# Distance factors of four batches at once on 32 partitions each, in a kernel of two graph layers with layernorms

## The reference, cut to what matters

```
s = x @ w_se.T + b_se                      # 512 x 3 for each batch
sq = sum(s * s, axis=-1)
dist = sq[:, :, None] + sq[:, None, :] - 2 * einsum('bnd,bmd->bnm', s, s)
A = exp(-dist) * mask
x_nmp = einsum('bnm,bmd->bnd', A, relu(x @ w_msg.T + b_msg))
```

## Time and profile before

| | |
|---|---|
| runs | 359.60, 358.53, 354.52 us; median 358.53 us |
| the profiled execution | 354.5 us, of it the span 352.4 us |
| PE busy | 335.6 us, 95% |
| DVE busy | 316.2 us, 90% |
| ACT busy | 237.3 us, 67% |
| DMA queue q1 | 33.49 MB, 31.1% of 16 engines' span |

### The profile page before, as it was taken

How to read it: one execution, slowest core, us unless ns; L and a number is a source line. 1 busy time by engine, 2 the same in 40 slices (tenths; PEclk the granted TensorE clock), 3 DMA queues, 4 the chain that set the end, 5 groups by cost and what they waited for, 6 DMA issues and landing times. The chain is left out here.

```text
span 352.4 us, 6224 instructions
## 1 busy us (share of the span) xinstructions
PE 335.6 (95%) x1769; PEld 274.6 (78%) x1769; DVE 316.2 (90%) x553; ACT 237.3 (67%) x409; POOL 93.2 (26%) x151
## 2 busy tenths in 40 slices
PE   4889999999999999999999999999999999999891
PEld 1577778987889688977989688977898688967580
DVE  2999999999999999999999999999999999987633
ACT  4382675748856696748865796659684885967842
POOL 4740001605050502323050504141140406050222
PEclk9989999999999999999999999999999999999998
DMA  6913341514044222604162312603161403421012
GB/s 183 327 24 119 91 138 46 173 32 150 19 114 147 64 88 56 195 25 149 31 182 63 121 33 72 198 20 129 45 201 30 149 17 93 139 74 37 0 32 60
DMA packets 31096, 34.00 MB, mean 96 GB/s; under 512 B 4919, under 2 KB 18271, under 8 KB 31079
## 3 DMA queue, kind: packets, MB, share of 16 engines
q1 hardware_dynamic: 30054, 33.49, 31.1%
q10 hardware_dynamic: 1024, 0.30, 0.3%
HBM read 24.85 MB, written 4.46 MB: 83 GB/s over the span
## 5 line engine op out<-in xcount | busy, mean ns | idle before, releaser
L1319 POOL TENSOR_TENSOR base<-mv,vscale 128x4 f32<-128x4 f32 x16 | 7.0, 437 | 232.3 <-DVE mv L1448 225.5
L715 PE MATMUL p_outer<-t_h,w_l 128*128 128x344 f32 x131 | 41.1, 330 | 0.6 <-DVE w_l L1526 0.6
L715 PE MATMUL p_outer<-t_h,w_h 128*128 128x344 f32 x131 | 41.0, 328 | 0.2 <-DVE rz L1523 0.2
L1416 DVE TENSOR_TENSOR am<-am,adj 128x512 f32<-128x512 f32 x64 | 39.9, 683 | 0.0
L1582 DVE TENSOR_TENSOR am_l<-am,am_h 128x2048 fp32r<-128x2048 f32 x15 | 34.3, 2286 | 1.8 <-ACT am_h L1172 1.8
L715 PE MATMUL p_middle<-t_h,w_h 128*128 128x344 f32 x90 | 28.6, 329 | 0.0
L1172 ACT ACTIVATE am_h<-am 128x2048 fp32r<-128x2048 f32 x15 | 28.5, 1901 | 0.0
L715 PE MATMUL p_middle<-t_h,w_l 128*128 128x344 f32 x90 | 28.0, 322 | 0.0
L715 PEld LDWEIGHTS p_outer<-t_h,w_h 128*128 128x128 f32 x131 | 24.3, 188 | 2.5 <-issue 0.6
L715 PEld LDWEIGHTS p_outer<-t_h,w_l 128*128 128x128 f32 x131 | 25.0, 195 | 1.2 <-DVE w_l L1526 0.9
L1131 ACT ACTIVATE yoo<-yn,nb,rs 128x128 f32<-128x128 f32 x63 | 25.9, 484 | 0.0
(11 more groups left out here) (381 smaller groups left out, 1010.0 us busy)
## 6 DMA issues: line engine op xcount, KB each, us to landing
adj<-adjT SPq DMA_DIRECT2D x64, 256.0 KB, 3.5
xpad<-xT SPq DMA_DIRECT2D x17, 256.0 KB, 3.1
out<-yoo SPq DMA_DIRECT2D x16, 256.0 KB, 2.3
crossed<-left SPq DMA_DIRECT2D x31, 48.0 KB
left<-left SPq DMA_DIRECT2D x30, 48.0 KB
right<-left SPq DMA_DIRECT2D x30, 48.0 KB
wc<-w_c SPq DMA_DIRECT2D x2, 384.0 KB, 6.6
wraw<-g_w SPq DMA_DIRECT2D x1, 640.0 KB
```

The lines of the kernel that those rows point to most:

```text
L715: return nc.tensor.matmul(out_, w, x, start=start, stop=stop, skip_group_check=True)
L1319: TT(base[:, 0:CH], mv[:, :, 1], vscale[:, 0:CH], ALU.mult)
L1416: TT(am[:, c, :], am[:, c, :], adj[:, c, :], ALU.mult).then_inc(s_am[c], 1)
```

## The change

1. **Rows.** One contraction now has KD = 30 rows, arranged so that the right side is the left side with its two halves of 15 rows exchanged. Only one side is computed, on 32 partitions for a batch, so four batches fit into 128 partitions. `rows` issues one matmul of 32 columns for each batch. In the head it makes batches 0 and 1, in batch 1 batches 2 and 3 (partitions 64 to 127), and in batches 3, 7 and 11 the next four. Batches 5, 9 and 13 no longer have `rows`, `rows_factor`, `rows_val`, `rows_high` or `rows_left`. For the two batches whose x isn't in `xin` yet, SP loads x a second time into `xr` (2 x 256 KB, in batches 2, 6 and 10).
2. **Right side.** DVE makes the right side by a stream shuffle of `left` within each 32 partitions into `crossed` (which is the memory of `val`), after `x_l` in an odd batch, five times in all.
3. **Distances.** `dist` uses two row quarters, the batch's own and its neighbour's, in turn: matmuls 0 and 2 on one, 1 and 3 on the other. SP issues three copies for each batch instead of six: one of the left rows, two of the right rows after the shuffle. Copies for the third and fourth batch of a group of four are issued in the next two batches.
4. **Head.** The `rowb` operation moves behind the steps of the first convolution. Batch 0 gets its right side through the shuffle and an ACT copy (`rights[0]`) instead of a DMA. On the ACT queue the two DMAs of `brow` become one.

```
-KD = 24
+KROW = 15
+KD = 2 * KROW
+MIRROR = [(r + KROW) % KD if r < KD else r for r in range(32)]
...
+            def spread_factors(v, event=None):
+                g, p = v % 4, v % 2
+                rows_l, rows_r = full(left[32 * g:32 * g + KD, :]), crossed[32 * g:32 * g + KD]
+                sp.dma_start(full(lefts[p][32 * other(g):32 * other(g) + KD, :]), rows_l).then_inc(s_right[p], 16)
+                if event is not None:
+                    after(sp, s_crossed, event)
+                for h in (g, other(g)):
+                    sp.dma_start(full(rights[p][32 * h:32 * h + KD, :]), rows_r).then_inc(s_right[p], 16)
...
-                if v % 2 and before(b, B - 2):
-                    after(sp, s_left, n.pair(1))
+                if v == 2:
+                    after(sp, s_rows, n.quad(0))
                     for q in range(2):
-                        spread_factors(q)
+                        sp.dma_start(xr[:, q, :], xT[b + 4 + q, :, :]).then_inc(s_xr, 16)
+                if v == 3 or static(b, 1):
+                    after(sp, s_left, n.quad(0)); after(sp, s_d, n(1))
+                    spread_factors(v + 1, n.quad(0))
+                    spread_factors(v + 2)
+                elif not isinstance(b, int):
+                    if v != 2:
+                        after(sp, s_d, n(0))
+                        spread_factors(v + 2)
...
+            def row_group(g, x_):
+                return mm(p_gh[32 * g:32 * g + 32, :], wrow[:], x_)
+
+            def rows(v, extra=False):
                 for q in range(2):
-                    last = mm(p_gh[64 * q:64 * q + 64, :], wrow[:], xin[:, (v + q) % 4, :])
+                    last = row_group((v + q) % 4, xin[:, (v + q) % 4, :])
+                if extra:
+                    for q in range(2):
+                        last = row_group(2 + q, xr[:, q, :])
                 last.then_inc(s_rows, 1)
...
-                at, other = 64 * (v % 2), 64 - 64 * (v % 2)
-                for c, (lhs, rhs, row) in enumerate(((left, crossed, at), (crossed, left, at + 32),
-                                                     (left2, right2, other), (left2, right2, other + 32))):
-                    last = mm(banks[c][:], lhs[row:row + KD, D * c:D * c + D], rhs[row:row + KD, :])
+                for c in range(CH):
+                    g, p = v % 4, v % 2
+                    h, lhs, rhs = other(g) if c % 2 else g, lefts[p] if c % 2 else left, rights[p]
+                    last = mm(banks[c][:], lhs[32 * h:32 * h + KD, D * c:D * c + D], rhs[32 * h:32 * h + KD, :])
                 last.then_inc(s_d, 1)
...
+            def rows_crossed(at, e):
+                nc.vector.stream_shuffle(crossed[at], full(left[at, :]), MIRROR).then_inc(s_crossed, 1)
...
-                dve.wait_ge(s_brow, 32); dve.wait_ge(s_cst, 16)
-                TS(rowb[:], brow[:], cst[:, C_ROW:C_ROW + 1], cst[:, C_ROW + 1:C_ROW + 2], ALU.mult, ALU.add).then_inc(s_rowb, 1)
...
-                rows_val(o, 0)
-                rows_left(o, 0)
+                dve.wait_ge(s_brow, 16); dve.wait_ge(s_cst, 16)
+                TS(rowb[:], brow[:], cst[:, C_ROW:C_ROW + 1], cst[:, C_ROW + 1:C_ROW + 2], ALU.mult, ALU.add).then_inc(s_rowb, 1)
+                rows_val(slice(0, 64), 1, 0)
+                rows_left(slice(0, 64), 1, 0)
+                dve.wait_ge(s_left, 1)
+                rows_crossed(slice(0, 64), 1)
...
+                    if v == 3 or static(b, 1):
+                        rows_left(part_of(v), n.quad(0), n(1))
+                        after(dve, s_left, n.quad(0))
                     x_low(v, n, 3)
+                    if v == 3 or static(b, 1):
+                        rows_crossed(part_of(v), n.quad(0))
                     inner_low(n)
```

More of the change, by code:

```diff
@@ L33 @@
 XS = N3 + 1
[L37 removed]
+KROW = 15
+KD = 2 * KROW
+MIRROR = [(r + KROW) % KD if r < KD else r for r in range(32)]
 def dist_rows():
[L42 to L55 removed]
+    first, second = [], []
+    for k in range(3):
+        first += [(k, 0.0, 1.0, 0), (k, 0.0, 1.0, 0), (k, 0.0, 1.0, 1), (k, -1.0, 0.0, 0), (k, -1.0, 0.0, 1)]
+        second += [(k, 0.0, 1.0, 0), (k, 0.0, 2.0, 1), (k, 0.0, 1.0, 1), (None, 0.0, 1.0, 0), (None, 0.0, 1.0, 0)]
+    return first + second, []
 (V_G1, V_B1, V_M1, V_V1, V_G2, V_B2, V_M2, V_V2, V_IR, V_IZ, V_IN, V_HR, V_HZ, V_HN) = range(14)
@@ L86, in constants @@
     c[:, C_ID:C_ID + D] = np.eye(D)
-    for side, rows in enumerate(dist_rows()):
-        for r, (_, alpha, beta, low) in enumerate(rows):
-            for b in range(2):
-                c[64 * b + 32 * side + r, C_ROW:C_ROW + 3] = alpha, beta, -low
+    for r, (_, alpha, beta, low) in enumerate(dist_rows()[0]):
+        for g in range(4):
+            c[32 * g + r, C_ROW:C_ROW + 3] = alpha, beta, -low
     c[:, C_ONE] = 1
@@ L586, in x_count, with other, part_of @@
             return (b - (v + k) % 4) * 4 + 16
+        def other(g):
+            return g + 1 - 2 * (g % 2)
+        def part_of(v):
+            return slice(64, 128) if v == 1 else slice(0, 128)
         def static(b, value):
@@ L937, in odd @@
                     g_pe.combine(pe, mm)
-                if more:
-                    after(pe, s_val, n.pair(1))
+                if v == 3 or static(b, 1):
+                    after(pe, s_val, n.quad(0))
                 after(pe, s_ghb, n(0)); gate(p_gh, "n", 2, xb_h, xb_l, True, True).then_inc(s_gx, 1)
@@ L1092, in first @@
                 act.wait_ge(s_rowb, 1)
-                act.wait_ge(s_rows, 1)
-                A(ab, p_gh[:], ACT.Identity, bias=rowb[:, 0:1], scale=cst[:, C_ROW:C_ROW + 1]).then_inc(s_ab, 1)
-                act.wait_ge(s_val, 1)
-                A(val_h[:], val, ACT.Copy).then_inc(s_valh, 1)
+                rows_factor(slice(0, 64), 1)
+                rows_high(slice(0, 64), 1)
                 middle_high(o)
```

101 lines of the change are left out of this document (45 added, 56 removed).

## The result

The two kernels were compared in 20 runs each. The median is 356.98 us after the change (356.08 to 361.75) against 354.89 us before (354.07 to 359.60); the ratio of the compared runs is 1.0054 with a 95% interval of [1.0031, 1.0076].

What follows compares the result with a forecast made beforehand. PE was taken to set the time, with DVE close behind. Rows -3.6 + 1.1, distances 2.5 + 1.5, shuffle 1.2 and head 1.0 made +3.7 us: 358.2 or 362.2, stated as 360.2, range 355 to 366.

Steps and rivals of the forecast that it cites:

- rows, batches 5, 9, 13: These batches lose a 1.21 us slot: 3 x 1.21 = 3.6 us saved, of which 1.1 us is lost again.
- shuffle, batches 3, 7, 11: 0.65 us of DVE each, also in batch 1; stalls PE 0.3 at the last convolution sum, 4 x 0.3 = 1.2.
- head itself: In the head, DVE's chain with the moved rowb and the shuffle makes the w_l of 21.28 come 1.0 us late.
- the distances' term: dist on two quarters: eight instances outside the even batches cost 0.31 each, 2.5 us; seven even ones 0.22, 1.5 us.
- So PE sets the time: In the loop PE sets the time with almost no slack; DVE's gains are worth nothing where PE is later.
- the rival of rounds that don't overlap: In dist the second round costs a whole slot of 0.43, 1.8 us more: 360.0 and 364.0; chance 0.06.
- quarters used in turn run one by one: Slow rival: dist costs 0.77, 6.9 us more than summed: 365.1 and 369.1; chance 0.07.
- the wait at L1461's successor: Sign expected in batches 3 and 4: PE waits 0.3 us for DVE at the last convolution sum.
- PE is full behind it: In the head, behind the w_l matmul of 21.28, PE has no pause, so w_l's 1.0 us delay counts.
- The two bases: The sum gives 358.2 on the profiled execution of 354.5, 362.2 on the median of 358.5; the middle, 360.2, is stated.

Runs made afterwards that it cites:

- a_rows_every: Changed kernel with two unused 32-column rows matmuls put back at the start of batches 5, 9 and 13; 359.86 us, ratio 1.0146 to the kernel before.
- b_two_quarters: Kernel before with only the distance matmuls changed, to use two row quarters in turn; 355.67 us, ratio 1.0008.
- a_no_shuffle: Changed kernel without DVE's shuffle, right sides made by SP's half copies, also in the head; 355.55 us, ratio 0.9996 to the kernel before.

## Why the prediction was right or wrong, point by point

The prediction forecast a small loss of 1 to 6 us, stated as 360.2 us, and named +3.7 as its sum. Measured is a small loss of 1.9 us in the span (354.3 - 352.4) and 2.1 between the medians. Direction, kind and range hold; the size of the loss is half, and it came even that near by luck, since the place of the half clock, which the forecast put at nothing, may have added as much as 0.88 us.

| term | forecast, us | measured, us | from |
|---|---|---|---|
| rows, batches 5, 9, 13 | -3.6 + 1.1 = -2.6 | -2.29 | a_rows_every less after |
| distances, batches 3 to 14 | 6 x 0.31 + 6 x 0.22 = +3.2 | +0.96 | b_two_quarters less before |
| shuffle, batches 3, 7, 11 | 3 x 0.3 = +0.9 | +1.56 | after less a_no_shuffle |
| sum of the middle stretch | +1.5 | +0.23 (measured whole +0.17) | |
| head itself | +1.0 | +0.16 | neighbour product, 31.02 against 30.86 at full clock |
| distances in the head | +0.31 | +0.23 | b_two_quarters |
| distances and shuffle, batches 1 and 2 | 0.31 + 0.22 + 0.3 = +0.83 | +0.41 | 39.97 against 39.56, from the first convolution of batch 1 to that of batch 3 |
| place of the half clock | 0 | +0.88 | 1.52 less 0.64, below |
| sum up to batch 3 | +2.1 | +1.68 | 85.70 against 84.02 |
| tail | 0 | +0.1 | |

The three single effects of the middle stretch add up to what it shows within 0.06, so none of them is badly mis-measured. The +0.41 is rough, as `rowb` moved in the kernel before gives 39.89 there with the loop unchanged. Without the half clock's place the change costs at least 0.17 + 0.16 + 0.23 + 0.41 + 0.1 = 1.1 us; it may be up to half a microsecond more, as said under the head.

**The failed step is the distances' term, "The eight instances outside the even batches [...] cost 8 x 0.31 = 2.5" and "with 0.22 it is 1.5 us".** For the twelve instances of the middle stretch it makes 3.2 us, and 0.96 was found. Three parts of it were mis-sized:

- The slot grows by 0.22 on average, not 0.31, which is 1.1 us less for twelve: two rounds of 0.33 stand against one of 0.43 or 0.44.
- The wait for c_l in even batches, which the term counted at 0.09 each (0.31 less 0.22), swallowed 0.16 each, 0.4 us more in six. The prediction had read 0.18 in batch 4.
- That PE waits for DVE anywhere else was put at nothing, and 0.7 us came back there: 0.3 at the convolution sums of batches 6 and 10, 0.25 ahead of the distances of batch 14, the rest in small pieces. The prediction read the turn in batch 4 alone, 109.17 and 109.22. There PE indeed has neither slack nor a wait (0.36 from the transposes, 108.86, to the stream). But batches 2, 6 and 10, which no row shows, wait 0.13 to 0.22. "So PE sets the time" holds in odd batches, where the slot is paid in full; in even ones DVE sets it, by the sum or by c_l.

The other prices that the prediction gave for this term can be ruled out. A whole second slot, 0.43, by which the rival of rounds that don't overlap was made, isn't there: the rounds are 0.33 apart and the slot is 0.67, not 0.86. The Trainium skill, "TensorE: Matmul & The Clock Gate", section "The mechanism" of part 3, says that a weight load overlaps running matmuls only on another row quarter; this trace does not agree, since the third and fourth matmul have the quarters of the first and second and add 0.23, which is also the distance of full matmuls. Nor do quarters used in turn run one by one (0.31 + 0.23 + 0.23); each round is one step.

**The shuffle** was right in duration (0.65 forecast, 0.73 found) and place (the wait at L1461's successor, four times), and yet costs 0.52 a time where 0.3 stood. The forecast was 0.65 of DVE less 0.31 by which PE is late through `dist`, less the lead of 0.05. Found are 0.87 of DVE, since the wait for `left` comes with the shuffle, and 0.30 to spare for PE without it, which would leave 0.57; 0.48 to 0.51 was measured at the stream. The 1.1 us in four that the view of waits gives looks like the 4 x 0.3 of the forecast, but it hides about 0.24 of each. The prediction's estimate from the Trainium skill, "VectorE: DVE Perf Modes", "The perf-mode tier table", was 0.6; the trace, with 0.72 to 0.73, is above it by a fifth.

Distances and shuffle meet at the same place: most of the 0.30 that PE has to spare in batch 4 without the shuffle is the longer slot of batch 3, since the kernel before had nothing to spare there.

**Rows** held: 1.19 us for four strips, 0.24 from gates to convolution in batch 5, and 0.42 given back where 0.35 stood. The places hold as well: the neighbour product waits 0.16 for `mt` (0.15 to 0.20 forecast), and the stream behind it 0.30 for ACT's part of `t_h` (0.15 forecast).

**The head** went wrong in a step, too, and the clock covered it. Timeline of the changed head, DVE and PE:

```profile
10.34 0.28 DVE L1542 TENSOR_SCALAR rowb<-brow,cst 128x1 f32<-128x1 f32 x1
...
11.47 0.74 DVE L1391 SCALAR_TENSOR_TENSOR rows<-p_gh,brow,rows 64x512 f32<-64x512 f32 x1 [0.84 <-ACT rows L1043]
...
14.40 0.67 DVE L1436 TENSOR_TENSOR mt<-p_z,bmsg 128x512 f32<-128x512 f32 x1
...
14.99 1.24 DVE L1550 SCALAR_TENSOR_TENSOR gtn<-wc 128x768 f32<-128x768 f32 x1
...
21.67 1.23 PE L733 MATMUL p_outer<-t_h,w_l 128*128 128x344 f32 x6 [0.60 <-DVE w_l L1559]
```

`val` starts at 11.47, to the hundredth as forecast, and `mt` 1.12 late (14.40 against 13.28). But w_l's matmul starts at 21.67, only 0.39 late against 21.28, because the weight sum of L1550 takes 1.24 us where the same operation took 1.97 before (by the timelines it runs less beside POOL, which was not tested). And the claim that "PE is full behind it" was wrong. In the kernel before it looked so, because PE ran its next three groups in the half clock (21.4 to 24.8, the third slice of the earlier trace rows and not the fourth). The kernel with two quarters has the same head up to the first distances of batch 1 and ran it at the full clock. Timeline of its PE:

```profile
24.99 1.19 PE L715 MATMUL p_middle<-t_h,w_h 128*128 128x344 f32 x6 [0.81 <-DVE rz L1531]
```

PE waits another 0.81 for DVE there, so DVE sets the time of this stretch. That group starts at 24.99 here, at 25.62 in the kernel before and at 25.17 after the change; the neighbour product of batch 0 behind it at 30.86, 31.50 and 31.02. So, read across single executions, the change delays the head by 0.16, and the half clock had delayed the kernel before by 0.64, the rest of its cost being hidden in that wait. After the change the half clock lay in the gates of batch 1, where PE alone sets the time, and cost 1.52 there: from the neighbour product to the first convolution of batch 1 it is 14.71 us (45.73 - 31.02) against 13.19 (44.05 - 30.86). The 0.88 between is in the two profiled executions. A part of it comes back: PE later waits for `mt` in batch 1, 0.44 us in the kernel before and 0.57 with two quarters (0.79 and 0.92 from transposes to neighbour product, where 0.35 is enough), and not at all after the change. How much of this is the clock's was not tested. Whether the twenty runs have it on average, and whether the change moves the stretch, is open: 2.1 us between the medians speaks for it, the lower end of the interval, 0.31% or 1.1 us, needs none of it.

**The two bases.** I had put the stated time half on the median of three runs, 358.5. On the profiled execution the sum gave 358.2, and 356.1 was found; on the twenty-run median it would have given 358.6 against 356.98. The sum is too high by 1.6 to 2.1 us; the rest of the 3.2 by which 360.2 missed comes from a median of three that spread over 5 us.

## What to carry to other kernels

When a matmul starts some 0.05 us behind its operand's end, PE has no slack there, but whether and how long it waited is not in that number, and the bracket can hide 0.24 us of a wait. Compare the distance of two starts with the same distance where nothing is waited for, and do it in several batches: one even batch without a wait stood for seven here, of which three had one. A cost on one engine is paid where that engine is the later one and swallowed where it is not, so lay two kernels side by side, start against start, before calling a term lost or kept; and expect a second cost of the same kind at its full duration, as with the second shuffle. And before an operation is moved because its operand is late, ask why the operand is late: here a plain source for one small transfer did more than the move, and a copy that DMA makes anyway was cheaper than an operation on DVE.

## What the runs showed of the hardware

**Half clock.** The granted clock falls to 0.5 (1.2 of 2.4 GHz) in short stretches whose place differs between the profiled executions: before at 21.4 to 24.8, after at 39.5 to 42.9, with two quarters not in the head at all but for 10 us near 340 (so its tail is 34.2 us instead of 29.9, and its profiled execution 359.5 us against a median of 355.7). The windows view of the kernel after (bounds, us, busy us and count of PE, PEld, DVE, ACT and POOL, granted clock, DMA share, GB/s):

```profile
36.00:44.00 8.00, 8.00 (x40) 6.11 (x39) 7.93 (x17) 4.75 (x9) 0.00 (x0) 0.79 0.08 17
85.70:324.30 238.60, 237.61 (x1265) 200.25 (x1262) 225.91 (x378) 170.57 (x287) 57.85 (x86) 1.00 0.30 93
```

and of the kernel before:

```profile
36.00:44.00 8.00, 8.00 (x48) 5.80 (x46) 7.71 (x17) 5.11 (x10) 0.00 (x0) 1.00 0.30 82
```

In the changed kernel 40 matmuls fit between 36 and 44 where 48 did. PE had been busy without a pause for over 8 us when its clock fell at 39.5; with `rowb` early it had run no matmul for some 5 us when the clock fell near 15. I can't say what sets the place. Such a stretch costs what PE loses less what it would have waited anyway, here 1.52 (before anything comes back later) and 0.64. Differences under 2 us between two executions are therefore to be read in a stretch at the full clock, as above.

**DVE beside POOL.** The same step of 128 x 356 elements took 0.63 us alone and 2.11 beside POOL's additions of 128 x 768. The Trainium skill, "SBUF — State Buffer", section "SBUF: two separate sides", has DVE operations with two SBUF inputs and POOL's contend for one port pair, the later one blocked until the earlier ends; the trace fits this: POOL's operation starts first, at 14.54, and ends at 16.69, and DVE's, which starts at 15.06, ends 0.48 behind it. No run here varies it.

**A repeated DMA source.** Half a KB for 128 partitions from 32 rows read four times over lands about 9 us after the start of its issue, the same from 64 plain rows by two DMAs in 4.6 to 6.3. The Trainium skill, "DMA: Bandwidth & Descriptors", section "Rules for kernel authors", says that a leading broadcast of c copies confines a DMA to at most c engines. The runs agree with that in kind, since a repeated source is late and a plain one is not, but no view of them shows engines singly, and whether there are two or four copies made no difference: `rowb` starts at 11.42 and 11.50.
